# A two-layer graph network on one core: the prologue's row statistics in parts of three, three and four chunks

## The reference, cut to what matters

```
h = max(layernorm(x), 0)
# layer 0
edge_feat = concat(h[src], h[dst], edge_attr)          # 40000 x 1088
m   = mish(mish(edge_feat @ W1 + b1) @ W2 + b2)        # mish(z) = z * tanh(softplus(z))
agg = segment_sum(m, dst)                              # 1250 x 512
u   = mish(concat(h, agg) @ W3 + b3) @ W4 + b4
x   = x + layernorm(h + u) * gamma + beta
# layer 1
h   = max(layernorm(x), 0)
s   = ((h @ U) * s) @ Vt                               # rank 64
x   = x + relu(segment_sum(s[src] * edge_weight, dst) + bias)
```

## Time and profile before

| | |
|---|---|
| median of three runs | 1541.91 us |
| the profiled execution | 1540.79 us |
| its span | 1539.1 us |
| TensorE busy | 1498.8 us (97%) |
| VectorE busy | 1414.7 us (92%) |
| ScalarE busy | 1296.5 us (84%) |
| GpSimd busy | 1082.4 us (70%) |
| prologue, up to the last matmul of table B | 0 to 76.7 us of the span |

### The profile page before, as it was taken

One profiled execution on the slowest core, in us unless ns is written; L12 is line 12 of the kernel. 1 busy time (PEld: TensorE's weight loads), 2 busy tenths in 40 slices (PEclk: granted clock), 3 DMA queues, 4 the chain that ended last, 5 costly groups with the idle time before them and its releaser, 6 DMA issues.

```text
span 1539.1 us, 33365 instructions
## 1 busy us (share of the span) xinstructions
PE 1498.8 (97%) x7862; PEld 1170.1 (76%) x7862; DVE 1414.7 (92%) x2922; ACT 1296.5 (84%) x2505; POOL 1082.4 (70%) x984
## 2 busy tenths in 40 slices
PE   7969999999999999999999999999999999999998
PEld 5747777777777777777777777777777777776785
DVE  7679999999999999999999999999999999995666
ACT  4058999999999999999999999999999999995462
POOL 1246888888888788787788887888878888762220
PEclk9979999999999999999999999999999999999999
DMA  8845555555554555544554555555555455455673
GB/s 310 306 138 142 125 118 122 124 119 117 124 123 116 123 123 115 127 117 115 126 119 116 127 121 117 121 124 118 118 122 124 116 123 124 112 136 127 137 146 151
DMA packets 122452, 205.10 MB, mean 133 GB/s; under 512 B 31641, under 2 KB 54297, under 8 KB 122416
## 3 DMA queue, kind: packets, MB, share of 16 engines
q0 software_dynamic: 59392, 116.85, 34.8%
q1 hardware_dynamic: 62672, 87.30, 18.2%
q10 hardware_dynamic: 352, 0.52, 0.1%
HBM read 151.60 MB, written 42.75 MB: 126 GB/s over the span
## 4 chain that ended last, share of the span: by engine, by line
PE 81%; issue 5%; DVE 4%; POOL 4%; DMA 3%; ACT 1%; POOLq 1%; DVEq 0%; SPq 0%; ACTq 0%
PE bm L1070 48%; PE bp L1049 6%; PE bp L1057 5%; PE bs L1093 4%; PE bp L1059 4%; PE pu L336 2%; PE pm L1081 2%; PE pu L1998 2%; PE po L2020 2%; PE pB L679 2%; DMA xg<-A_tab,idx 1%; PE pm L1080 1%; POOL hTl L974 1%; POOL M_tab L999 1%; POOL agg_tab L988 1%
## 5 line engine op out<-in xcount | busy, mean ns | idle before, releaser
L974 POOL TENSOR_TENSOR hTl<-tp,hTh 128x512 fp32r<-128x512 f32 (+1 forms) x314 | 411.0, 1309 | 224.5 <-DVE khl L1261 203.5
L1070 PE MATMUL bm<-W2h,hTh 128*128 128x512 f32 x1252 | 498.4, 398 | 2.2 <-POOL hTl L974 1.7
L1070 PE MATMUL bm<-W2l,hTh 128*128 128x512 f32 x1252 | 497.0, 397 | 0.0
L1070 PE MATMUL bm<-W2h,hTl 128*128 128x512 f32 x1252 | 494.5, 395 | 0.0
L963 POOL DMA_INDIRECT xg<-A_tab,idx x305 | 319.4, 1047 | 49.5 <-issue 39.1
L1070 PEld LDWEIGHTS bm<-W2h,hTh 128*128 128x128 f32 x1252 | 235.5, 188 | 71.7 <-DVE bm L1254 14.8
L1131 ACT ACTIVATE rp<-bp 128x512 f32<-128x512 f32 (+1 forms) x314 | 183.3, 584 | 116.8 <-PE bp L1059 115.7
L1070 PEld LDWEIGHTS bm<-W2l,hTh 128*128 128x128 f32 x1252 | 235.6, 188 | 57.5
L1070 PEld LDWEIGHTS bm<-W2h,hTl 128*128 128x128 f32 x1252 | 235.6, 188 | 53.7
L1225 DVE SCALAR_TENSOR_TENSOR rp<-rp 128x512 f32<-128x512 f32 (+1 forms) x314 | 215.6, 687 | 38.7 <-ACT rp L1131 25.8
L1235 DVE SCALAR_TENSOR_TENSOR tp<-rp,bp 128x512 f32<-128x512 f32 (+1 forms) x314 | 211.7, 674 | 4.5 <-ACT rp L1137 2.2
(11 more groups left out here) (244 smaller groups left out, 2318.9 us busy)
## 6 DMA issues: line engine op xcount, KB each, us to landing
ea<-in_eaT SPq DMA_DIRECT2D x156, 128.0 KB
M_tab<-mev POOLq DMA_DIRECT2D x157, 80.0 KB
agg_tab<-ev POOLq DMA_DIRECT2D x157, 64.0 KB
db<-in_dst_rows SPq DMA_DIRECT2D x78, 128.0 KB
M<-M SPq DMA_DIRECT2D x76, 128.0 KB
xg<-A_tab,idx POOLq DMA_INDIRECT x313
eaW<-Bh_tab SPq DMA_DIRECT2D x77, 64.0 KB
eaW<-Bl_tab SPq DMA_DIRECT2D x77, 64.0 KB
```

The costliest lines, as they stand in the source:

```text
L974: e.tensor_tensor(hTl[p][:, j, 0:w], pick(u, start_t, tp)[:, 0:w], hTh[p][:, j, 0:w], ALU.subtract)\
L1070: last = e.matmul(bank[0:r, :], a[p][:, c, j * P:j * P + r], w[:, c, :], start=False, stop=c == KC - 1 and w is W2l, skip_group_check=True)
```

## The change

`BATCH` goes from parts of two, three and five chunks to three, three and four. With it the loads of `x` have other sizes, and ScalarE takes logarithm and exponential of the second part at chunk 3 in place of 2, and of the third at chunk 5 in place of 4. On VectorE `windows` goes from behind chunk 2 to behind chunk 1, the variances of the third part from behind chunk 1 to behind chunk 2, its `scales` from behind chunk 3 (ahead of `iotas`) to behind chunk 4 (ahead of `w1_hi`), and `columns` from behind chunk 8 to behind chunk 9.

```
-BATCH = [(0, 2), (2, 5), (5, NCH)]
+BATCH = [(0, 3), (3, 6), (6, NCH)]
...
-                between = {0: [lambda: variances(1), lambda: scales(1)], 1: [lambda: variances(2)], 2: [windows],
-                           3: [lambda: scales(2), iotas], 4: [lambda: w1_hi(1)], 5: [lambda: w1_lo(1)], 6: [w2_hi],
-                           7: [w2_lo], 8: [columns], 9: [bases]}
+                between = {0: [lambda: variances(1), lambda: scales(1)], 1: [windows], 2: [lambda: variances(2)],
+                           3: [iotas], 4: [lambda: scales(2), lambda: w1_hi(1)], 5: [lambda: w1_lo(1)], 6: [w2_hi],
+                           7: [w2_lo], 9: [columns, bases]}
...
-                        if c == (0, 2, 4)[i]:
+                        if c == (0, 3, 5)[i]:
```

## The result

The changed kernel is slower. Its median is 1545.32 us (10 runs, 1544.5 to 1549.91), against 1541.62 us for the kernel before (10 runs); the ratio is 1.0029, 95% interval 1.0020 to 1.0038, so 3 to 6 us. A second measurement, made beside the experiments, gave 1545.52 us against 1541.23 and a ratio of 1.0028 (1.0018 to 1.0039). The forecast was 1541.2 with a range from 1538.6 to 1544.1.

A forecast was written before the change was run, and what follows sets the result against it. TensorE's chain was taken as the bound, the prologue counting only through table B's start. Terms 1.35 - 0.25 - 1.0 + 0.4 + 0.15 - 1.4 = -0.75 us gave a median of 1541.2 us, range 1538.6 to 1544.1.

The forecast's parts named there:

- First part of three chunks: Prologue start: 256 KB more to load (0.7 us) and one more bn_stats (0.6) make chunk 0 come 1.35 us later.
- the bound of 1.45: Upper bound, in us, on how much later everything up to table A's chunk 0 comes; the lower was 0.6.
- Logarithm behind `ta`: ScalarE's second-part logarithm after chunk 0's `ta`: new TensorE wait of about 1.4 us near 18, chunk 1 at 19.4.
- `windows` and the third variances swapped: VectorE behind chunks 1 and 2: `windows` ends at 21.9, chunk 2's 1.0 us loss goes, chunk 3 loses 0.5.
- the 0.75 us early: Forecast sum of all prologue terms: table B starts at 47.9 us in place of 48.64.
- The third rival: TensorE's clock falls at the new 1.4 us wait; twenty slowed matmuls cost 4.8 us, time 1546.0; chance 0.06.
- the 0.5 that I had lost there: Table A's chunk 3: its `nTl` ends at 26.35 behind four chunks' variances, TensorE ready at 25.88; 0.5 us lost.
- W2: W2's load, issued 1.1 us later at 23.65, lands at 35.6 to 36.7; chunks 7 and 8 lose 0.15 us.
- The first rival: Prologue length doesn't move: W2 lands at 37.4 and the gain is spent there; 1541.9 us, chance 0.28.
- the far bound: Latest W2 landing, 39.6 us, with another megabyte (2.9 us) in front of it; time 1544.1 us.
- the second rival: Edge stage's earlier start spares the low-clock stretch at 111 to 120 us, winning 2.9 us more; 1538.3, chance 0.06.
- `columns` behind chunk 9: End of table A: chunk 9 no longer waits for VectorE's `columns`; 1.4 us won.

The follow-up runs named there:

- changed_again: The changed kernel measured once more beside the experiments, nothing altered; 1545.52 us, ratio to the kernel before 1.0028.
- swap_only: Kernel before with only `windows` moved behind chunk 1 and the third part's variances behind chunk 2; 1548.88 us, ratio 1.0047.
- windows_back: Changed kernel with variances put back behind chunk 1 and `windows` behind chunk 2; 1540.73 us, ratio to the kernel before 0.9998.
- targets_split: Changed kernel with the target rows loaded in two loads of 64 and 15 rows; 1541.16 us, ratio to the kernel before 1.0002.
- columns_first: Changed kernel with the target columns' load issued ahead of the target rows' load; 1546.34 us in one run.
- columns_late: Kernel before with only `columns` moved from behind chunk 8 to behind chunk 9; 1540.21 us, ratio 0.9996.
- zeros_late: Changed kernel with GpSimd's zero stores to the aggregation table issued four chunks later; 1540.44 us in one run.
- best_order: Kernel before, parts unchanged, with target rows in two loads, third part's bn_stats spread, `windows` behind chunk 4, W1/W2 splits and `columns` one chunk later; 1539.91 us, ratio 0.9988.

## Why the prediction was wrong, point by point

The table goes from each chunk's `nTl` matmul to the next, in us. Its last column adds up to the 3.7 us by which table B missed the forecast (51.62 against 47.9).

| step | before | forecast | measured | measured less forecast |
|---|---|---|---|---|
| chunk 0's time | 12.35 | 13.7 | 14.28 | +0.58 |
| to chunk 1 | 5.93 | 5.7 | 5.85 | +0.15 |
| to chunk 2 | 4.23 | 3.25 | 5.78 | +2.53 |
| to chunk 3 | 3.34 | 3.75 | 4.92 | +1.17 |
| 4 to 6 | 9.78 | 9.7 | 9.69 | -0.01 |
| 7 and 8 | 6.84 | 7.0 | 6.45 | -0.55 |
| to chunk 9 | 4.19 | 2.8 | 2.78 | -0.02 |
| to table B | 1.98 | 2.0 | 1.87 | -0.13 |

*First part of three chunks: mis-sized.* The 256 KB cost 1.26 us (5.67 against 4.41) and not 0.7: I divided by the rate that all transfers together have. The half of W1 behind it landed 7.0 us after its issue and not 6.3, the 0.7 that the division gives for both together; so the likely reason is that the two are served at once and the first part gets only a share of the rate. No run tests that. The bn_stats was 0.6 as said. In all 1.93 us, above the bound of 1.45.

*Logarithm behind `ta`: right.* Sum, place and size of the wait (1.44) are as worked out.

*`windows` and the third variances swapped: this is the step that failed.* I priced `windows` at its own 2.63 us and put it at 19.27, and never asked whether what it waits for was there. In the trace before, it ran at 22.48 without a wait, and that says only that its loads had landed by 22.48. The landing was the unknown of the step: the wait was put at nothing and got no bound, where the trace before left anything from nothing to 22.48 - 19.27 = 3.2 us. With that end the 0.75 us early become 2.5 late, and the upper end of the range, 1544.1, becomes 1547.3, which holds the time. Measured were 2.47 us of wait in `windows` and 2.28 in front of TensorE. Even 3.2 was no true upper end, for the change moves the landing too: with the new parts the load landed at 22.5 to 23.9, and in changed_again the wait was 4.98. swap_only, windows_back and targets_split show that this is the cause; columns_first shows which of the two loads.

*The clock: the right mechanism at the wrong wait.* The third rival had TensorE's clock fall at the new wait of 1.4 us. It didn't there. It fell behind the wait of 2.28 us that I had not seen, and the slow stretch costs 4.92 - 3.23 = 1.7 us, with the 0.5 that I had lost there for another reason contained in it. So the loss in table B against the forecast is the wait, 2.5, the clock behind it, 1.2, and the first part, 0.6, less what chunks 7 and 8 gave back. In windows_back, which has the wait of 1.44 and not the other, no matmul behind 17 us is slow. It was put at twenty matmuls and 4.8 us; the stretch at 0.60 holds 12 instructions of TensorE, four of them transposes. The rival's time, 1546.0, is near the result by luck: it slows twenty matmuls at a wait that slowed none.

*W2: not late at all.* Its load was issued at 24.52, 1.9 us later than before and not 1.1, yet it landed 9.1 us behind that, at 33.6, where it was 35.6 before. `w2_hi` was reached at 38.54 and did not wait. The first rival, landing at 37.4, falls, and chunks 7 and 8 gave 0.55 us back. Why the load was quicker, 9.1 against 13.0 us, is open. The sum for the far bound had a slip besides: 2.7 above 1541.2 is 1543.9 and not 1544.1.

*The low clock at 111 to 120 us, the second rival.* It came with the edge stage, 3 us later: the clock reads 0.73 from 114 to 123 us in the changed kernel. Nothing was spared.

*`columns` behind chunk 9: right*, here and in columns_late.

*From table B to the end: 1491.6 in place of 1490.5.* The two profiled executions differ by 4.1 us, and 1.6 of them are not the prologue's: one group of 24 matmuls in the node stage took 7.38 us and 5.81 before, with the clock at 0.74 from 1485 to 1490 us and 1.00 before (chains of waits, the first of the changed kernel, the second of before):

```profile
1483.45 7.38 PE po L2020 x24
```

```profile
1480.89 5.81 PE po L2020 x24
```

windows_back has 7.38 here and targets_split 5.81, with medians 0.4 us apart. Such stretches of low clock come and go between kernels whose node stage is the same to the instruction, so an execution says little on one or two microseconds there.

## What to carry to other kernels

When an instruction that waits for a load is moved up, its old place gives only the latest time at which the load can have landed in that trace. The bound on the new wait reaches from nothing to the whole move at least, and the range has to hold it; a change that also alters the loads ahead can shift the landing and make the wait longer still. Look for a stretch in which the DMA engines are hardly busy while loads are outstanding: here that was one transfer on one engine, and splitting its rows in 64 and 15 cost one more issue. A gain in a prologue can be followed to the start of the next stage, and still shrink in the last stages, where a transfer or a clock level sets the pace.

## What the runs showed of the hardware that was not expected

- A load of 79 rows of 2 KB runs on one of sixteen DMA engines at 25 GB/s; 158 KB at that rate are over 6 us (an estimate from the two numbers; zeros_late shows five of them unmixed, from 13 to 18 us). Stores issued by GpSimd at the same time lengthen it (both loads landed at or before 20.2 us without them, at 22.5 to 23.9 with them).
- Loads issued by SyncE long after it are late too: with it in two loads, W2 landed 10.1 us behind its issue and not 13.0, the second half of W1 7.5 and not 11.1.
- A wait of 1.4 to 1.5 us did not lower TensorE's clock in any of these kernels; behind waits of 2.28, 3.95, 4.02 and 4.80 us for `nTl` of chunk 2 there were matmuls of up to twice the length. The length of one wait alone doesn't decide it: in best_order TensorE waited 2.50 us at 14.1 (for ScalarE's chunk 2), and what followed had its full pace. In columns_first the granted clock read 0.50 from 25 to 29 us, and TensorE stood still until 26.62: it fell during the wait.
- One profiled execution doesn't stand for the median within 2 us. targets_split started table B 2.1 us early in an execution that took 1538.91 us, 1.9 below that of the kernel before; its median is only 0.5 lower.
